# GpSimd adds the returned rows of three of eight batches, and each batch's returned rows get a buffer of their own

## What is computed

```
x = x + xattn(layernorm(x), ctx_1024, ...)
# _expert(x, up, down) = gelu(x @ up) @ down
probs = softmax(x @ router_w);  top_k_prob, top_k_idx = top_k(probs, 2)
gates = einsum('bsk,bske->bse', top_k_prob, onehot(top_k_idx))
routed_out = sum over e of gates[..., e:e+1] * _expert(x, routed_up[e], routed_down[e])
x = x + (_expert(x, shared_up[0], shared_down[0]) + routed_out + x_normed)
```

## Time and profile before

| | |
|---|---|
| median of three runs | 2335.02 us |
| the profiled execution's own time | 2343.26 us |
| its span, first to last instruction | 2341.6 us |
| busy: PE, DVE, ACT, POOL | 95%, 77%, 59%, 12% |
| mean granted TensorE clock | 0.98 of full |

### The profile page before, as it was taken

One profiled execution on the slowest core, in us unless ns is written; L12 is line 12 of the kernel. 1 busy time (PEld: TensorE's weight loads), 2 busy tenths in 40 slices (PEclk: granted clock), 3 DMA queues, 4 the chain that ended last, 5 costly groups with the idle time before them and its releaser, 6 DMA issues. The chain is left out here.

```text
span 2341.6 us, 40683 instructions
## 1 busy us (share of the span) xinstructions
PE 2223.5 (95%) x13782; PEld 1580.1 (67%) x13782; DVE 1801.9 (77%) x2413; ACT 1372.9 (59%) x2038; POOL 271.9 (12%) x302
## 2 busy tenths in 40 slices
PE   3999999999999999999999999999739999999997
PEld 3666665665666666666666565657628899999996
DVE  4899889899899898988989987895404555557776
ACT  4666666567567557666756755564214556567762
POOL 2010000000000000000000100002750111112110
PEclk9999999999999999999999999999859999999998
DMA  6235225324523523523442452234442344437756
GB/s 238 83 105 179 78 79 179 102 92 124 157 73 99 182 70 105 180 89 90 147 131 73 131 153 78 64 122 138 147 163 73 114 140 129 136 119 223 223 198 220
DMA packets 148990, 306.06 MB, mean 131 GB/s; under 512 B 34753, under 2 KB 71233, under 8 KB 145793
## 3 DMA queue, kind: packets, MB, share of 16 engines
q1 hardware_dynamic: 138688, 273.77, 37.9%
q0 software_dynamic: 10176, 30.45, 3.6%
HBM read 190.36 MB, written 79.20 MB: 115 GB/s over the span
## 5 line engine op out<-in xcount | busy, mean ns | idle before, releaser
L806 ACT ACTIVATE probs<-scores 128x1024 f32<-128x1024 f32 x512 | 504.0, 1024 | 203.8 <-PE scores L632 106.3
L1072 DVE TENSOR_TENSOR sums<-sums,probs 128x1024 f32<-128x1024 f32 x384 | 470.5, 1225 | 13.6
L676 PE MATMUL sum_ps<-probs,v_nat 128*64 128x512 f32 x2056 | 469.8, 599 | 1.1 <-DVE probs L970 1.1
L632 PE MATMUL scores<-q_split,k_split 64*128 64x512 f32 x3072 | 425.6, 409 | 0.1
L970 DVE TENSOR_SCALAR probs<-probs 128x2048 f32<-128x2048 f32 x256 | 313.3, 1224 | 140.3 <-ACT probs L806 139.6
L1654 PE MATMUL sum_ps<-down,hid_split 128*128 128x256 f32 x2640 | 362.1, 286 | 46.7 <-issue 38.2
L1654 PEld LDWEIGHTS sum_ps<-down,hid_split 128*128 128x128 f32 x2640 | 347.5, 194 | 67.1 <-issue 50.0
L632 PEld LDWEIGHTS scores<-q_split,k_split 64*128 64x128 f32 x3072 | 268.3, 184 | 158.0 <-issue 62.8
L1631 PE MATMUL scores<-xT,up 128*128 128x512 f32 (+1 forms) x1680 | 355.7, 353 | 12.2 <-issue 11.9
L1788 DVE TENSOR_TENSOR hid_split<-hid,hid_split 128x512 fp32r<-128x512 f32 x205 | 142.0, 692 | 278.4 <-ACT hid_split L1718 239.5
L1717 ACT ACTIVATE hid<-scores 128x512 f32<-128x512 f32 x220 | 131.3, 597 | 327.1 <-PE scores L1631 244.1
(11 more groups left out here) (201 smaller groups left out, 2309.5 us busy)
## 6 DMA issues: line engine op xcount, KB each, us to landing
k_two<-k_two SPq DMA_DIRECT2D x256, 128.0 KB, 2.3
w_all<-wpack SPq DMA_DIRECT2D x62, 512.0 KB, 4.4
raw<-L_ffn_routed_up SPq DMA_DIRECT2D x27, 1024.0 KB
raw<-L_ffn_routed_down SPq DMA_DIRECT2D x27, 1024.0 KB
rden<-rden_rows SPq DMA_DIRECT2D x128, 128.0 KB, 2.9
ctx_parts<-stage SPq DMA_DIRECT2D x28, 512.0 KB, 5.6
ctx_all<-ctx_parts SPq DMA_DIRECT2D x14, 1024.0 KB, 7.0
sorted_rows<-zero POOLq DMA_DIRECT2D x64, 162.5 KB, 2.8
```

Of the source, the lines that this page charges most:

```text
L632: last = pe.matmul(scores[j % 2][:, head], k_split[i][own, a, j * P:(j + 1) * P], q_split[i][own, m], start=n == 0, stop=n == 2)
L676: last = pe.matmul(sum_ps[64 * head:64 * head + 64, p % 2], v_nat[p // 2 % 2][:, j, cols:cols + 64], probs[:, j % PROBS, head], start=j == ...
L806: act.activation(probs[:, j % PROBS], scores[j % 2][:], ACT.Exp, scale=float(HD) ** -0.5).then_inc(s_exp, 1)
L1072: v.tensor_tensor(to, to, probs[:, j % PROBS], ALU.add).then_inc(s_add, 1)
```

## The change

- Each of the eight batches has a buffer for its returned rows: besides the old four, the four halves of the weight buffers `up` and `down` that the late tiles don't use (128x2048 each). SP issues all eight loads in a row, and then the stores in order of batch.
- GpSimd takes batches 1, 3 and 5: for each, eight multiplications by the gate (TENSOR_SCALAR, 128x256, in place) and then two additions to `acc[b]` (TENSOR_TENSOR, 128x1024).
- DVE keeps batches 0, 2, 4, 6 and 7: ten halves, which fill the ten places of `COMBINE`. Nothing of `combine` is left behind the last `hidden`.
- SP's store of a batch of GpSimd's waits for GpSimd, and the stores behind it with it.

```diff
-    gat = [t[:, 0:2 * QT * D].rearrange("p (t n d) -> p t n d", n=2, d=D) for t in pair + raw[1 - ROUTED % 2]]
-    GATS = len(gat)
+    whole = [t[:, 0:2 * QT * D] for t in raw[1 - ROUTED % 2][::-1] + pair]
+    split = [t[:, h].bitcast(F32) for t in (up[ROUTED % 2], down[ROUTED % 2]) for h in range(2)]
+    BY_POOL = (1, 3, 5)
+    BY_DVE = [b for b in range(B) if b not in BY_POOL]
+    gat = [None] * B
+    for b, t in zip([BY_DVE[0]] + list(BY_POOL) + BY_DVE[1:], whole + split):
+        gat[b] = t.rearrange("p (t n d) -> p t n d", n=2, d=D)
...
         for b in range(B):
-            if b >= GATS:
-                sp.wait_ge(s_half, 2 * (b - GATS + 1))
             src = ys[2 * (b * N + 1):2 * (b * N + N + 1)]
-            sp.dma_start(gat[b % GATS], src.rearrange("(p t n) d -> p t n d", p=P, n=2)).then_inc(s_gat[b % GATS], 16)
-            if b >= GATS:
-                store(b - GATS)
-        for b in range(B - GATS, B):
-            sp.wait_ge(s_half, 2 * (b + 1))
+            sp.dma_start(gat[b], src.rearrange("(p t n) d -> p t n d", p=P, n=2)).then_inc(s_gat[b], 16)
+        for b in range(B):
+            if b in BY_POOL:
+                sp.wait_ge(s_phalf, 2 * BY_POOL.index(b) + 2)
+            else:
+                sp.wait_ge(s_half, 2 * BY_DVE.index(b) + 2)
             if b == B - 1:
                 sp.wait_ge(s_comb, 1)
             store(b)
...
+        for i, b in enumerate(BY_POOL):
+            pool.wait_ge(s_gat[b], 16)
+            for n in range(2):
+                for t in range(QT):
+                    q = b * QT + t
+                    last = pool.tensor_scalar(gat[b][:, t, n], gat[b][:, t, n], gate[n][:, q:q + 1], None, ALU.mult)
+                last.then_inc(s_gated, 1)
+            for n in range(2):
+                pool.wait_ge(s_gated, 2 * i + 1 + n)
+                if n == 1:
+                    pool.wait_ge(s_phalf, 2 * i + 1)
+                pool.tensor_tensor(acc[b], acc[b], gat[b][:, :, n], ALU.add).then_inc(s_phalf, 1)
...
-                    for half in range(len(COMBINE), 2 * B):
-                        combine(half // 2, half % 2)
-                    v.wait_ge(s_half, 2 * B)
+                    assert len(COMBINE) == 2 * len(BY_DVE)
+                    v.wait_ge(s_half, 2 * len(BY_DVE))
                 shared_sum(t)
```

More of the change, by code:

```diff
@@ L1340, in experts @@
     s_back, s_free = sem("f_back"), sem("f_free")
-    s_gat = [sem(f"f_gat{i}") for i in range(GATS)]
-    s_half = sem("f_half")
+    s_gat = [sem(f"f_gat{b}") for b in range(B)]
+    s_half, s_gated, s_phalf = sem("f_half"), sem("f_gated"), sem("f_phalf")
     s_comb = sem("f_comb")
@@ L1937, in address, with combine @@
             v.tensor_tensor(dest[n.u][:, 0:q], whither[:, 0:q], aside[:, 0:q], ALU.add).then_inc(s_dest, 1)
-        def combine(b, n):
+        def combine(i, n):
+            b = BY_DVE[i]
             if n == 0:
@@ L1943, in combine @@
                     v.wait_ge(s_y, late(1).T)
-                v.wait_ge(s_gat[b % GATS], 16 * (b // GATS + 1))
+                v.wait_ge(s_gat[b], 16)
             else:
-                v.wait_ge(s_half, 2 * b + 1)
+                v.wait_ge(s_half, 2 * i + 1)
             for t in range(QT):
                 q = b * QT + t
-                last = v.scalar_tensor_tensor(acc[b][:, t], gat[b % GATS][:, t, n], gate[n][:, q:q + 1], acc[b][:, t], ALU.mult, ALU.add)
+                last = v.scalar_tensor_tensor(acc[b][:, t], gat[b][:, t, n], gate[n][:, q:q + 1], acc[b][:, t], ALU.mult, ALU.add)
             last.then_inc(s_half, 1)
```

## The result

Measured side by side on one chip, the changed kernel took 2346.28 us (median of five runs, 2341.21 to 2348.6) and the kernel before 2334.92 us (five runs, 2333.86 to 2338.68): a ratio of 1.0037, with an interval from 1.0023 to 1.0051. The prediction had 2335.5 us and a range of 2328 to 2341: the time lies outside it, on the slow side, and the change is clear of the 0.2% that the prediction took as the least that can be told from no change. A second comparison on another chip gave 1.0025 (1.0012 to 1.0038).

The account below looks back on a forecast made before the run. The prediction took the end to hang on DVE at two places, the middle and the last `shared_sum`. Its terms, -9.1 for the tail and +9.6 for the middle, gave +0.5 us: 2335.5 us, eight-in-ten range 2328 to 2341.

Parts of the forecast that it names:

- The tail, -9.1: Behind the last `hidden`: 24 of 28 DVE additions go, 10.0 us, of which 9.1 count since PE's end is late next.
- Loads, 0: SP's eight loads in a row: every batch lands before DVE wants it, and transfers don't slow DVE; cost 0.
- The size of a multiplication, 0.38 us: On GpSimd: 256 elements take 0.38 us, between 0.30 and 0.63, making GpSimd's whole work 25 us.
- The taking of turns: DVE and GpSimd alternate, one instruction each, up to the middle `shared_sum`; 2.25 us per addition, 0.14 per multiplication; chance 0.58.
- The middle, +9.6: At the middle `shared_sum`: four GpSimd additions cost 9.0 us, 16 multiplications 2.2, less 1.6 idle, so 9.6 us late.
- rival 2: Before the middle `shared_sum`: DVE's queued instructions go first, only two GpSimd additions fall ahead; -5.2 us, 2329.8; chance 0.16.
- Behind it PE sets the pace again ... Cost 0: Behind the middle `shared_sum`: PE sets the pace for 20.3 us, and GpSimd's remaining 5.2 us fit DVE's 6.5 idle; cost 0.
- GpSimd is done by about 2324: Near the end: GpSimd finishes its three batches at about 2324, ahead of the last `shared_sum`.
- The end, 0: At the end of the span: GpSimd is done before the last `shared_sum`, stores of batches 5 and 6 out in time.
- rival 3: At the end: DVE preferred, GpSimd ends about 2342 with stores behind it, deciding from 2335.5; +6.5 us, 2341.5; chance 0.16.

Follow-up runs that it names:

- e1: Changed kernel with all eight batches given back to DVE, keeping the eight buffers and the loads in a row; ratio to before 0.9993.
- e8: Changed kernel with one GpSimd multiplication of 128x1024 by constant 1.0 in place of four of 128x256; 2291.17 us, one execution, no ratio.
- e3: Changed kernel without GpSimd's 24 multiplications, so that it only does its six additions; ratio to before 0.9999.
- e0: The changed kernel once more, unaltered, beside the kernel before on another chip; ratio 1.0025.
- e7: Changed kernel with SP's store of batch 5 moved behind those of batches 6 and 7; ratio to before 1.002.
- e9: Kernel before, plus one 128x8 GpSimd MEMSET that waits for the last `shared_sum`; ratio to before 1.0027.
- e10: Changed kernel with GpSimd on batches 1 and 3 only, adding behind the middle `shared_sum`, and one DVE `combine` half moved behind that sum; ratio to before 0.9998.
- e2: Changed kernel without GpSimd's six additions, so that it only multiplies; ratio to before 0.9956.
- e4: Changed kernel with GpSimd multiplying by constant 1.0 in place of the gate's pointer, same shape; 2333.27 us, one execution, no ratio.

## Why the prediction was wrong, point by point

**The tail, -9.1.** Right as far as it goes: 24 of 28 additions went, and PE's end was next late. The last `shared_sum` came 0.76 us behind PE's end instead of 9.12.

**Loads, 0.** Right (e1). The landing of batch 1 was misread: the 6.2 us of the earlier trace rows is the median of two loads, and batch 1 is the second of the pair. GpSimd began 8.06 us behind the first load, where the prediction had 6.8.

**The size of a multiplication, 0.38 us: wrong, and the first step that failed.** It took 1.03. The rows I took it from, MEMSET and AFFINE_SELECT, priced it at 0.85 ns an element; e8 gives 2.59. The row beside them, L1564 with 1.295 us for 512 elements, has 2.53 ns an element, and the prediction had used it as the upper end, 0.63 (half of 1.295 is 0.65). One input isn't cheaper than two here: for 1024 elements it took 2.95 us and two took 2.54. Even that upper end was too low, by the fixed part of 0.30 us (the prediction had 0.08) and the pointer's 0.07. Everything on GpSimd's own path hangs on this price. With 0.38 it would have been done at about 2320 and its DRAIN, 9.1 us, would have been over before the end; with 1.03 it sets the end. The Trainium skill's GPSIMD Engine Reference, section Engine selection, holds that one-input work is roughly at line rate, by the prediction's estimate 0.21 us for 256 elements. Here 256 elements take 256 x 2.59 = 0.66 us beside the fixed part, some three times that, and the measurement decides.

**The taking of turns: right for additions, wrong for multiplications.** e3 shows it for the first. A GpSimd multiplication holds one DVE instruction for a part of its own length only: by 0.23 us (0.70 instead of 0.47) where it lasts 1.03, and by 0.79 (1.26) where it lasts 2.95 (e8). The other DVE instructions beside it aren't held. So the prediction's way of pricing it, its length less 0.24, would have charged 0.79 for a multiplication of 1.03, and two errors partly hid each other. The Trainium skill's SBUF — State Buffer, section Who interferes with whom, has the loser wait out the whole instruction. The additions here agree (2.82 us for a `hidden` of 0.69); the multiplications don't.

**The middle, +9.6: measured +4.8.** The additions did hold the middle back, as forecast. But 8 multiplications took 8.2 us, so only two additions came ahead of the middle `shared_sum`, not four. Two at 2.1 and 0.5 for the multiplications make 4.7. That the size came out as half was the long multiplication's doing, not DVE's preference as in rival 2: in e3, without multiplications, all six additions came ahead of it.

**"Behind it PE sets the pace again ... Cost 0": wrong, +5.4.** The step rests on "GpSimd is done by about 2324". It was done at 2337.59. (The idle time that the prediction set against its work was 3.79 and four times 0.54, 6.0 us, not five times; the 5.2 us would still have fitted.) Its last two additions fell on the last `hidden`, for which PE waited 2.95 us, and the last down product ran at a clock of 0.51: 4.4 us. The other 1.0 is the clock behind the middle stall, which the prediction had named and put at nothing. That part isn't shown to be the stall's: the 18 matmuls that took 4.42 us behind 1.98 us before and 5.26 behind 6.72 here took 4.20 and 4.47 behind 6.54 and 6.71 in e0 and e7. The last down product varies as well, 2.92, 2.33 and 1.90 us behind waits of about 3.0. None of it moved the end of the span, as the tails of 58.8 show.

**The end, 0: wrong, +2.9.** GpSimd became the end, as in rival 3, and its last addition did end behind rival 3's point (2337.59, or 2337.04 counted from before's first load, against 2335.5). But the mechanism was not the one named. SP's DRAIN stands 4.7 us behind the last `shared_sum` in both kernels, so the stores cost nothing. It was GpSimd's DRAIN, which ends 9.1 us behind its last instruction and which the prediction's sum doesn't have at all. Its row stood in the trace of before (9.2 us at 2288.0). e9 shows that a late GpSimd instruction is enough to bring it to the end.

**The sum.** Along DVE's and PE's work, -8.4 + 4.8 + 5.4 + 2.9 = +4.8 (rounded from +4.77) against +0.5. Of the error, -4.8 lies in the middle, +5.4 behind it, +0.8 in the part of the tail that was left, and +2.9 at the end. The terms partly cancelled, which was luck: the time missed by less than they did together.

**What stays open.** The profiled executions differ by 5.3 us, 0.23%, and the second comparison has 0.25%. The first has 0.37%, medians 11.4 us apart. The intervals overlap, and the traces show no further loss behind the first load; why the first is larger is not settled. Why a multiplication holds DVE for a part of its length and an addition for all of it isn't shown either, only that it is so.

## What to carry to other kernels

Price an operation on an engine by the nearest row that reads what it reads, and give a form that no row shows a range well above that row: here the row gave 0.65 us and the instruction took 1.03. Before giving an engine work near the end, look at what it still has to do behind its last instruction: here GpSimd's last instruction must end more than 9 us before the other engines are done, or it sets the end. Give GpSimd what hardly holds DVE at any time, and put what does where DVE has a gap and PE isn't waiting: the same two batches gave nothing with their additions ahead of the middle sum and 0.15% with them behind it. When such help has filled all of DVE's gaps, moving work about gains no more, as e10 showed.

## What the runs showed of the hardware

- GpSimd's closing DRAIN: 9.06 to 9.20 us where none of its other instructions ran any more (9197 ns in e9, 9198 ns before, 9060 ns in e2), whether it had last issued a scatter, multiplied or done a MEMSET. Started beside a running addition it takes 11.4 to 11.8 us (11742 ns in the changed kernel, 11447 in e4) and ends 9.1 us behind that.
- A GpSimd multiplication by a scalar, f32 in SBUF: 1.03 us for 128x256 with a pointer (0.92 beside an idle DVE), 0.96 with a constant, 2.95 for 128x1024 with a constant.
- Beside a GpSimd addition with two SBUF inputs a DVE instruction of 0.42 or 0.69 us takes up to 2.86 us. Beside a multiplication of 128x256 one takes 0.70 instead of 0.47, beside one of 128x1024 one takes 1.26, and the others keep their length.
- Behind waits of 6.72 and 2.95 us PE ran at 0.50 and 0.51 for 18 and 12 matmuls, in e0 behind 6.54 and 3.00 us at 0.65 and 0.66. In e10, behind waits of 0.42, 1.88 and 1.64 us, 12 down matmuls took 1.67 to 1.70 us at a clock of 1.00.
